# RWKV-style layer on one core: output projection and second transposed norm in the front PSUM banks, a buffer of their own for the normalised copy, projections in quarter steps, key blocks among the state application, new issue order

## The reference, cut to what is computed

```
xn = ln(x, ln1_w, ln1_b)
sx = token_shift(xn, state[:, i1])                      # previous token minus this one
xxx = tanh((xn + sx * maa_x) @ maa_w1) @ maa_w2         # five low-rank mixes
x5 = xn + sx * (maa_stack + xxx)
w = exp(-exp(time_decay + tanh(x5[1] @ decay_w1) @ decay_w2))
r, k, v, g = x5[3] @ Wr.T, x5[0] @ Wk.T, x5[2] @ Wv.T, silu(x5[4] @ Wg.T)
scan over tokens:  out = r . (u * k v + s);  s = k v + w * s
att = groupnorm(out) * gn_w + gn_b                      # per head
x = x + att * g @ Wo.T
xn2 = ln(x, ln2_w, ln2_b);  sx2 = token_shift(xn2, state[:, i0])
xk, xr = xn2 + sx2 * ffn_maa_k, xn2 + sx2 * ffn_maa_r
x = x + sigmoid(xr @ ffn_Wr.T) * (square(relu(xk @ ffn_Wk.T)) @ ffn_Wv.T)
```

## Time and profile before

| | |
|---|---|
| median of 3 runs | 795.35 us (793.9 to 798.16) |
| the profiled execution, its own time | 795.61 us |
| its span | 793.8 us, so 1.8 us lie around it |
| PE busy | 705.9 us, 89% |
| DVE, POOL, ACT busy | 513.6, 376.7, 324.7 us |
| granted TensorE clock, mean | 0.971 |
| DMA engines' share after the loads | about 1 to 2 tenths |

### The profile page before, as it was taken

How to read it: one execution, slowest core, us unless ns; L and a number is a source line. 1 busy time by engine, 2 the same in 40 slices (tenths; PEclk the granted TensorE clock), 3 DMA queues, 4 the chain that set the end, 5 groups by cost and what they waited for, 6 DMA issues and landing times.

```text
span 793.8 us, 17668 instructions
## 1 busy us (share of the span) xinstructions
PE 705.9 (89%) x7412; PEld 491.4 (62%) x7412; DVE 513.6 (65%) x767; ACT 324.7 (41%) x639; POOL 376.7 (47%) x223
## 2 busy tenths in 40 slices
PE   5986899997999889998799979998799978998797
PEld 4763677465674667556664665746665556755673
DVE  5638865695567774597556966677736965479441
ACT  2231843247332753427532483326433375325311
POOL 1248426763458435573257634584255732674000
PEclk9997899999999989999999999999999999999799
DMA  7910001010020201010010200202010000100000
GB/s 205 377 28 27 9 2 48 6 62 3 1 54 1 61 3 35 21 53 9 2 50 5 61 2 1 53 2 62 2 41 14 28 8 2 53 2 28 2 1 26
DMA packets 19275, 28.79 MB, mean 36 GB/s; under 512 B 5888, under 2 KB 11776, under 8 KB 18176
## 3 DMA queue, kind: packets, MB, share of 16 engines
q1 hardware_dynamic: 19200, 27.67, 11.0%
HBM read 18.35 MB, written 4.19 MB: 28 GB/s over the span
## 4 chain that ended last, share of the span: by engine, by line
PE 51%; issue 15%; POOL 14%; DVE 11%; ACT 7%; DMA 0%; POOLq 0%; DVEq 0%; ACTq 0%
PE FB L563 17%; PE BAB L820 7%; POOL pp L488 7%; PE FA L838 5%; PE FB L571 5%; PE FA L872 2%; ACT half L1048 2%; PE BAB L797 2%; PE FA L639 2%; DVE kvs L1357 2%; PE BAB L555 2%; PE FA L859 2%; PE BAB L733 2%; POOL mixes L453 2%; POOL mixes L451 1%
## 5 line engine op out<-in xcount | busy, mean ns | idle before, releaser
L488 POOL TENSOR_TENSOR pp<-rT,kT 128x2048 f32<-128x2048 f32 (+1 forms) x32 | 108.6, 3406 | 51.7 <-DVE rT L1229 51.7
L451 POOL TENSOR_TENSOR mixes<-mixes 128x1024 f32<-128x1024 f32 x30 | 72.0, 2400 | 127.9 <-ACT mixes L971 127.9
L453 POOL TENSOR_TENSOR mixes<-mixes,xnT 128x1024 f32<-128x1024 f32 x30 | 71.8, 2392 | 2.4
L563 PE MATMUL FB<-mixes,wk_s 128*128 128x256 f32 x256 | 66.1, 417 | 5.8 <-POOL mixes L453 3.5
L1321 DVE TENSOR_REDUCE half<-half 128x256 f32<-128x2048 f32 (+2 forms) x32 | 64.4, 2014 | 0.6
L504 POOL TENSOR_TENSOR acc<-acc,half 128x512 f32<-128x512 f32 x32 | 41.1, 1283 | 49.5 <-DVE half L1321 48.3
L563 PE MATMUL FB<-mixes,wv_s 128*128 128x256 f32 x256 | 60.8, 382 | 2.5 <-issue 1.5
L563 PE MATMUL FB<-mixes,wg_s 128*128 128x256 f32 x256 | 62.1, 392 | 0.0
L563 PEld LDWEIGHTS FB<-mixes,wk_s 128*128 128x128 f32 x256 | 52.1, 208 | 15.9 <-POOL mixes L453 4.5
L971 ACT ACTIVATE mixes<-FA,cols_s 128x256 f32<-128x256 f32 x116 | 45.4, 481 | 38.4 <-PE FA L639 33.4
L838 PE MATMUL FA<-wide,fk_s 128*128 128x256 f32 x256 | 57.2, 381 | 3.5 <-DVE wide L1472 2.2
(11 more groups left out here) (160 smaller groups left out, 1336.7 us busy)
## 6 DMA issues: line engine op xcount, KB each, us to landing
pp<-x SPq DMA_DIRECT2D x8, 512.0 KB, 3.8
xt<-x SPq DMA_DIRECT2D x8, 512.0 KB, 3.8
vp<-vT SPq DMA_DIRECT2D x128, 32.0 KB, 1.9
out<-wide SPq DMA_DIRECT2D x7, 512.0 KB, 3.0
wv_s<-wv SPq DMA_DIRECT2D x1, 1024.0 KB, 5.1
wk_s<-wk SPq DMA_DIRECT2D x1, 1024.0 KB, 7.6
wr_s<-wr SPq DMA_DIRECT2D x1, 1024.0 KB, 8.7
wg_s<-wg SPq DMA_DIRECT2D x1, 1024.0 KB, 10.8
```

The lines of the kernel that those rows point to most:

```text
L451: nc.gpsimd.tensor_tensor(slot, slot, sx, ALU.mult).then_inc(s_["mixm_ready"], 1)
L453: nc.gpsimd.tensor_tensor(slot, slot, xnT[:, :, 1:L + 1], ALU.add).then_inc(s_["mix_ready"], 1)
L488: ins = nc.gpsimd.tensor_tensor(pp[:, i % 2, 0:size].rearrange("p (n i j) -> p n i j", i=m, j=m), spread(r.unsqueeze(3), 3, m), spread(k.u ...
L563: ins = nc.tensor.matmul(dst[:, c * L:(c + 1) * L], weight[:, q, c * P:(c + 1) * P], src[:, q, :], start=(q == 0), stop=(q == C - 1))
```

## The change

It does six things:

1. `b_wo` and `b_norm2` on PE write FA instead of BA and BB; their readers on DVE and ACT read FA. For that, the first `b_wo` matmul waits until ACT has taken the next sample's last mix out of FA (`mixe_ready`), `b_norm2` waits until both halves of x1 are added, and the first `c_fk` matmul waits until ACT has read all four channel tiles of the turned norm (`xn2T_ready`). POOL's `b_prod0` gets a wait on `y1_ready`.
2. `xhat2` gets 4 KB per partition of its own.
3. `c_fk` is cut into four steps (by input tile), `c_fr` and `c_fv` into four each, `b_wo` into four; the matmuls are the same in number and shape.
4. In the main stages `f_k2` and `f_k3` (PE) move from behind the state application into it.
5. The four tables have a new order on PE, POOL and ACT (DVE's only in `last`).
6. The filling matmuls of the last stage (`warm`) write FB and wait for `vexp_ready`.

The core of the diff:

```
-            c_fk b_score0 c_fr0 c_fr1 b_score1 c_fv0 b_score2 c_fv1 b_g0 b_score3 f_norm b_g1 b_score4 b_g2 b_g3
+            c_fk0 c_fk1 c_fk2 b_score0 c_fk3 c_fr00 c_fr01 c_fr10 c_fv00 b_score1 c_fv01 c_fv10 b_score2 c_fr11
...
-        xhat2 = cen
+        xhat2 = sb("xhat2", [P, T, E])
...
                     if i == 0 and not first(b):
+                        pool.wait_ge(s_["y1_ready"], C * b)
...
-                    for q, t in (((0, 0), (0, 1), (1, 0), (1, 1), (2, 0), (3, 0)), ((2, 1), (3, 1)))[part]:
+                    for q, t in (((0, 0), (0, 1)), ((1, 0), (1, 1)), ((2, 0), (3, 0)), ((2, 1), (3, 1)))[part]:
                         if t == 0:
                             pe.wait_ge(s_["y_ready"], C * b + q + 1)
-                        ins = nc.tensor.matmul(BA[:, t * E:(t + 1) * E], ...
+                        if q == 0 and t == 0:
+                            if last(b):
+                                pe.wait_ge(s_["mul_ready"], T * b)
+                            else:
+                                pe.wait_ge(s_["mixe_ready"], NMIX * (b + 2))
+                        ins = nc.tensor.matmul(FA[:, t * E:(t + 1) * E], ...
-                    ins.then_inc(s_["wo_ready"], 1)
+                    if part >= 2:
+                        ins.then_inc(s_["wo_ready"], 1)
...
-                    transpose_channels(BB, xhat2, [t]).then_inc(s_["xhat2T_ready"], 1)
+                    if t == 0:
+                        pe.wait_ge(s_["x1_ready"], T * b + T)
+                    transpose_channels(FA, xhat2, [t]).then_inc(s_["xhat2T_ready"], 1)
...
+            def c_fk(q):
+                def run(b, par, n):
+                    if q == 0:
+                        loaded("fk")
                     pe.wait_ge(s_["xk_ready"], C * b + q + 1)
+                    if q == 0:
+                        pe.wait_ge(s_["xn2T_ready"], C * b + C)
...
+            def token_half(dst, weight, src, t, h):
+                for q in (2 * h, 2 * h + 1):
+                    ins = nc.tensor.matmul(dst[:, t * E:(t + 1) * E], src[:, q, t * P:(t + 1) * P], big[weight][:, q, :],
+                                           start=(q == 0), stop=(q == C - 1), skip_group_check=True)
+                return ins
...
-                            dve.wait_ge(s_["xhat2T_ready"], T * b)
+                            dve.wait_ge(s_["nrmT_ready"], T * b)
```

More of the change, by code:

```diff
@@ L52 @@
         first="""
-            f_norm warm6 f_lora1 f_lora0 f_pair1 f_m20 f_k0 f_k1 f_k2 f_k3 f_dec1 f_pair3 f_v0 f_v1 f_dec2 f_v2
-            f_v3 f_r0 f_r1 f_r2 f_r3""".split(),
+            f_norm warm6 f_lora1 f_lora0 f_pair1 f_m20 f_k0 f_k1 f_k2 f_dec1 f_pair3 f_k3 f_v0 f_v1 f_v2 f_v3
+            f_r0 f_r1 f_dec2 f_r2 f_r3""".split(),
         second="""
-            b_score0 f_norm b_g0 b_score1 b_score2 b_score3 b_g1 b_score4 b_g2 b_g3 b_vtok f_lora0 f_lora1
-            b_ktok f_m20 b_kv0 b_kv1 f_m21 f_dec1 f_m22 f_dec2 b_acc b_apply0 b_apply1 f_k0 b_apply2 b_apply3
@@ L58 @@
-            f_k1 f_k2 f_v0 f_k3 f_m23 f_v1 b_gn0 b_gn1 f_v2 b_wo0 f_m24 b_wo1 f_r0 b_norm20 f_v3 f_r1 f_r2
-            b_norm21 f_r3""".split(),
+            b_score0 b_score1 b_g0 f_norm b_score2 b_score3 b_g1 b_score4 b_g2 b_g3 b_vtok f_lora0 f_lora1
+            b_ktok f_m20 b_kv0 b_kv1 f_dec1 f_m21 f_dec2 f_m22 b_acc b_apply0 f_k0 b_apply1 b_apply2 f_k1
+            b_apply3 f_m23 f_k2 f_v0 b_gn0 f_m24 f_v1 b_gn1 f_k3 f_r0 b_wo0 b_wo1 b_wo2 b_wo3 f_v2 f_r1 f_v3
+            b_norm20 b_norm21 f_r2 f_r3""".split(),
@@ L60 @@
         main="""
-            c_fk b_score0 c_fr0 c_fr1 b_score1 c_fv0 b_score2 c_fv1 b_g0 b_score3 f_norm b_g1 b_score4 b_g2 b_g3
-            b_vtok f_lora0 f_lora1 b_ktok f_m20 b_kv0 b_kv1 f_m21 f_dec1 f_m22 f_dec2 b_acc f_k0 f_k1 b_apply0
-            b_apply1 b_apply2 b_apply3 f_k2 f_k3 f_v0 f_m23 b_gn0 f_v1 b_gn1 f_v2 b_wo0 f_m24 b_wo1 f_v3 f_r0
-            f_r1 b_norm20 f_r2 b_norm21 f_r3""".split(),
+            c_fk0 c_fk1 c_fk2 b_score0 c_fk3 c_fr00 c_fr01 c_fr10 c_fv00 b_score1 c_fv01 c_fv10 b_score2 c_fr11
@@ L65 @@
+            c_fv11 b_score3 b_g0 f_norm b_g1 b_score4 b_g2 b_g3 b_vtok f_lora0 f_lora1 b_ktok f_m20 b_kv0 b_kv1
+            f_m21 f_dec1 f_dec2 f_m22 b_acc f_k0 f_k1 b_apply0 f_k2 b_apply1 b_apply2 f_k3 b_apply3 f_m23 f_v0
+            f_m24 b_gn0 b_gn1 f_v1 f_v2 f_r0 b_wo0 b_wo1 b_wo2 f_v3 b_wo3 f_r1 b_norm20 f_r2 b_norm21 f_r3""".split(),
         last="""
-            c_fk b_score0 c_fr0 b_score1 c_fr1 b_g0 b_score2 b_g1 b_g2 b_score3 b_g3 c_fv0 b_score4 b_vtok c_fv1
-            b_ktok b_kv0 b_kv1 warm14 b_acc b_apply0 b_apply1 b_apply2 b_apply3 warm8 warm20 b_gn0 b_gn1 b_wo0
```

93 lines of the change are left out of this document (50 added, 43 removed).

## The result

The changed kernel takes 840.35 us (median of 4 runs, 837.54 to 844.18) against 795.72 us (4 runs, 793.90 to 798.16): ratio 1.054, 95% interval 1.050 to 1.058. The forecast was 840. The profiled execution took 837.54 us, the least of the four, its span 835.7.

What follows compares the result with a forecast made beforehand. PE's own work, busy 89% of the span, was taken as the floor, with its waits on top. 795.6 + 39.0 (six main stages) + 6.8 (second) - 1.3 (last) = 840 us; range 794 to 849.

Steps and rivals of the forecast that it cites:

- The root: Group norm's inverse root on DVE, main stages: POOL's mix 3 multiply and add hold it twice, +2.9 us a stage.
- no collision: Rival: POOL's waiting multiply does not get in, or mix 3 comes later than the root; 803 us, chance 0.10.
- the third: Rival of filled gaps: score 0 costs nothing, keys fill the application's holes, root runs clean; 787 us, chance 0.18.
- Keys among the application: Key blocks within the state application, main stages: issue pauses go, but the squares start later, +1.6 us a stage.
- Score 0: Start of a main stage: PE reaches score 0 earlier and stalls 1.6 us for its operand; sum +1.3 us.
- An earlier issue waits for the same end: Start of a stage: POOL's product, even if issued earlier, waits until DVE's six back-to-back instructions end; PE stalls 1.6 us.
- its last rival: Gaps filled: POOL's score product gets in at once, DVE's 0.5 us gate wait is gained; 787 us, chance 0.18.
- Scaling to the next stage and clock: Main stage's end: new order -0.6 us; half clock for about 3 us after PE's 5.8 us pause +1.3 us.
- the order's term: From scaling to the next main stage: new order, mix 4's matmuls ahead of the first transpose, -0.6 us a stage.
- Main stage: Sum of all terms for one of the six main stages: +6.5 us, six of them +39.0.
- Second stage: Collision +2.4, keys among the application +1.6, longer list behind it +1.5, clock +1.3: +6.8 us.
- The last stage and the tail: Last stage: two half steps of c_fv and two DVE multiplies leave the state's way, -1.3 us; tail 0.

Runs made afterwards that it cites:

- run 4: Changed kernel with key blocks f_k2 and f_k3 of the main stages put back behind the state application: 830.7 us, ratio 1.042.
- run 8: Changed kernel with POOL's mix 3 held until the root is done and ACT's last main-stage steps in their old order: 803.03 us, ratio 1.006.
- run 1: Changed kernel with one wait more: POOL starts mix 3 (multiply and add) only when the root is done: 797.86 us, ratio 1.001.
- run 2: Changed kernel with 20 unused matmuls ahead of the group norm's transposes in the second and main stages: 817.59 us, ratio 1.025.
- run 5: Changed kernel with only the add of POOL's mix 3 held until the root is done, its multiply not: 823.45 us, ratio 1.032.

## Why the prediction was right, point by point

*The root*, +2.9 forecast, +2.94 measured. Two holds, on the instructions of the two-input forms. They fell on two neighbours, the fifth and sixth in four stages and the fourth and fifth in two, where the fifth and seventh were forecast: no instruction passed between them. (Had only the scalar form been held, the sum would have been the 803 of "no collision", the second rival and not the third.) The Trainium skill (SBUF — State Buffer, section "Who interferes with whom") has two-input DVE instructions and GpSimd reads exclude each other, the first issued keeping the other out; the 2.31, 2.21 and 2.27 us of these forms, against 0.225 clean, agree.

*Keys among the application*, +1.6 forecast, +1.60 measured: 7.11 us, and no pause over 0.2 us among them in any main stage, while taking the blocks out again brought pauses back in all six (run 4). What was weighed against it in the prediction, the Trainium skill (Runtime: NRT & Kernel Launch, section "Instruction fetch mechanics"), tells of blocks of 256 instructions and calls a crossing mostly hidden. The spacing of 127 matmul records with as many weight loads, 254 in all, agrees with the block. That it is hidden the rows of 1.1 to 2.4 us contradict where small matmuls stand close together; where long ones stand between, as here, at most 0.2 us of a pause is left (0.7 in one stage of run 8).

*Score 0*, +1.3 forecast, -0.5 measured. This step failed. "An earlier issue waits for the same end" took it that POOL cannot get in among DVE's six back-to-back instructions. In the stage shown POOL's product is now issued 1.0 us after S instead of 2.45, 0.36 us into the six, and it got in; in five of the six stages it came 0.4 to 0.6 us into them and got in. Run 8 shows the other half: issued 2.25 us after S it waits, and the stall of 1.52 us is there. Even then most of the stall was taken up before the application (0.3 us left), so the part given back was under-estimated too. The prediction named this outcome as a bound (0) and, with the 0.5 us gained, in its last rival.

*Scaling to the next stage and clock*, -0.6 + 1.3 = +0.7 forecast, +1.58 measured. Without the clock loss, run 1 gives 23.62 - 24.03 = -0.4 and run 2 -0.5, so the order's term (-0.6) was nearly right and the clock's was too small: 25.61 - 23.53 = 2.1 us where 1.3 was put. I had read 3 us at half clock off the first pause of the trace, one of 3.4 us; after a pause of 5.6 us it was nearly 7, of which PE worked 5.6.

*Main stage*: +6.5 forecast, +5.59 measured. Two errors (1.8 too much, 0.9 too little) half cancel.

*Second stage*, +6.8 forecast, +10.3 measured. The collision came as forecast (root 7.17 against 4.58: +2.6 for +2.4). The application ended 3.75 us later instead of 1.6: the first key block's wait for POOL's mix (0.9) and its half clock (1.4) were not in the sum. From scaling to the first main stage it was +3.9 for the +2.8 of the longer list and the clock. The last stage and the tail: -1.3 forecast, -1.9 measured.

So the cause was right: two holds of about 2 us and the half clock behind them are the loss. The total, 840 against a median of 840.35 (837.54 for the profiled execution), is closer than the terms deserve: 39.0 + 6.8 - 1.3 was 33.5 + 10.3 - 1.9. The main stages came out 5.5 us too high and the second stage 3.5 too low, and the median lies 2.8 us above the profiled execution; that these met is luck.

## What to carry to other kernels

Before moving a POOL instruction forward, look at what DVE does at the time it will be *issued*. Here each POOL instruction of 2.2 to 2.3 us beside a chain of short, semaphore-linked DVE instructions cost the chain 2 us, and one wait on the chain's end was worth 5% of the kernel. Count a pause of PE together with what stands behind it. And do not add up the effects of single moves: here mix 2, mix 3, the keys and the fillers change each other's effect, because each shifts who meets whom.

## What the runs showed of the hardware

- Who waits in a collision can turn on a microsecond of issue time. POOL's product issued 0.36 us into DVE's six back-to-back instructions ran in 2.35 us, and they took 5.81; issued 1.6 us into them it took 3.09, and they took 2.46. Over the main stages of the kernel before, the changed one and run 8, it got in wherever it came 0.4 to 0.6 us into the six, and waited for their end wherever it came 1.6 us or more into them.
- PE's pauses named issue in dense small matmuls stand 127 matmul records apart (behind 101 and 228 of the application here, 106 and 233 or 124 and 251 in the kernel before) and move with the code in front of them, one record per record to within two. Moving them by matmuls that do nothing, so that one of about 1.2 us is left instead of two of about 2, took 4.6 to 4.8 us from the last stage, clock included, more than the forecast size of most edits. A difference of this size between two kernels can be the place of the code alone.
- Ahead of the transposes the clock stayed at 2.4 GHz behind PE's pauses of 0.6 to 1.8 us in run 1, and fell to 1.2 GHz in or right behind those of 2.7 to 3.8 us in run 5 and of 4.6 to 5.8 us in the changed kernel, in all six main stages of each. The stretch from scaling to next S lost 1.8 us in run 5 and 2.0 in the changed kernel. The length of the pause alone does not decide it: in run 8 the clock fell behind 1.65 and 1.70 us and stayed behind 1.69.

Open: why POOL gets in among DVE's six early and not late; what the pause named issue ahead of the second stage's application waits for; where the rest of the 10.3 us up to the first main stage goes; and why only one of the two pauses due in the shifted application shows.
